# Two-layer conditional attention block on one core: the second layer's token eviction, ten groups' maxima and the last batch's tangent order move between ACT, DVE and Pool

## The chip, the cores and the metric

The kernel runs on one core of a Trainium2 chip. The metric is the device time of one execution in microseconds (us); the lower the better. The profile and the trace come from one profiled execution.

## What is computed

Four batches of 512 tokens with 256 channels pass through two attention layers of 16 heads (16 channels a head). Cut to what matters:

```python
# layer 0: RMS norm, modulation, rotary attention, output projection, residual
xn = x * rsqrt(mean(x * x) + eps) * rms_w
qkv = (xn * (1 + scale) + shift) @ w_qkv
x = softmax(rope(q) @ rope(k).T / 4) @ v @ w_out + x
# layer 1: layer norm, attention with a key mask, then a modulated second norm
xn = layer_norm(x, norm_w, norm_b)
y = softmax(q @ k.T + (1 - mask) * -1e6) @ v
e = silu(emb) @ emb_w + emb_b                      # scale, shift = halves of e
h = layer_norm(y, sb_norm_w, sb_norm_b) * (1 + scale) + shift
x = x + silu(h) @ out_w + out_b
```

`silu(h)` is computed as `(tanh(h/2) + 1) * (h/2)`. The change touches how `h/2` and `tanh(h/2)` are made for the four batches of the second layer.

## The kernel before, in words

**Steps and tiles.** The attention is cut into 32 groups (layer, batch, four heads): groups 0 to 15 are the first layer, 16 to 31 the second. Step s works on group s, and has four key tiles k = 0 to 3. Within a key tile the order of all engines is written out in `KEY_TILE`: the scores and the shifts of four heads (PE into one of four banks, ACT exponentiates into `probs`, L707), four row maxima of group s+2 (PE L524 makes row scores into one of three banks, DVE reduces them, L854 in the second layer), and the values product of the tile before (PE L541, eight records in a key tile). In key tile 1 PE also turns the maxima of group s+1 (L549), in key tile 2 it turns the output of group s-1 (L556), which DVE divides (L879, L881). Steps 30 and 31 have no row maxima, for there is no group 32.

**Rings.** What ACT evicts goes through the ring A of four banks, what DVE evicts through the ring D of three. A place in a ring is counted by `places()` in the order in which work is written out, and PE may fill the bank of a place once the place four (A) or three (D) before is evicted (`a_free`, `d_free`). All engines work through their own instructions in order.

**Pieces.** Other work is placed by hand in `PIECES`. In steps 22, 26 and 30, in key tiles 0 and 1, PE turns the normalised output tokens of batch 0, 1 and 2 of the second layer (`("turn", "f1", b, h)`, four transposes each, L576). Before the change they go into ring A, and ACT evicts each bank twice: with Identity into `halved` (L745, h/2), and with Tanh into `tanh` (L746), both with a scale and a bias per partition. (`halved` and `tanh` lie in the memory of `tables`, which is the name that the profile gives them.) Pool then makes `(tanh + 1) * halved` (L1245, L1247). PE projects it one step later (`y` pieces, L615), and DVE adds the residual (L903).

**Maxima to shifts.** Once the 16 maxima of a group are there, `negate` scales them by -1/64 and splits them into a high and a low part: on DVE in two instructions (L865, L867), on Pool in three (L1232, L1235, L1237). `POOL_SHIFTS` lists the groups for which Pool does it. The maxima of group n are complete at the end of step n-2; PE turns them in key tile 1 of step n-1, ACT copies them (L720), and DMA brings them to where step n uses them. In step 20, 24 and 28, key tile 3, DVE also takes the statistics of the output (L887, L892), and Pool makes the reciprocal deviation and the normalised tokens from them (L1089, L1091, L829).

**The last batch.** Behind the last step, batch 3 is done in two pairs p of token tiles by code of its own: ACT takes Tanh of each half bank (L789, four), DVE waits for each and then makes `halved` (L1024) and the product (L1027) from it, PE projects (L654), DVE adds (L1033). PE fills its waits with idle matmuls (L630).

Of the kernel before, what the change touches and what calls it, by code (L numbers as in the profile page):

```python
# [51 lines left out]
def spread(pieces):  # L52

    table = {}
    for step, by_tile in pieces.items():
        for k, names in enumerate(by_tile):
            table[step, k] = names
    return table
# [70 lines left out]

FIRST_BUSY = 14  # L130
LAST_BUSY = (14, 7)
PIECES = spread(PIECES)


# [20 lines left out]
TURNED = 1  # L155


POOL_SHIFTS = [23, 24, 25, 27, 28, 29, 31]


PARTS_AT = {-1: ((1, 0), (1, 1)), 0: ((1, 2), (1, 3)), 2: ((2, 0), (2, 1)), 3: ((2, 2), (2, 3)),
# [51 lines left out]
def places():  # L213

    a, d = {}, {}
    for entry in order():
        op = entry[0]
        if op == "score":
            a[entry] = len(a)
        if op == "maxima":  # L220
            a["shift", entry[1]] = len(a)
        if op in ("max", "output"):
            d[entry] = len(d)
        if op == "piece":
            ring = d if entry[1][0] in ("y", "modulate", "embed") else a
            ring[entry[1]] = len(ring)
    return a, d

# [12 lines left out]


def turned(use):
    return A[("turn",) + use + (CT - 1,)] + 1


def await_read(engine, q, use):
# [27 lines left out]
def columns(p):  # L275

    return slice(2 * p * P, (2 * p + 2) * P)
# [23 lines left out]
def build(nc, x, condT, mask, tables, vecs, w_cond, w_qkv, w_out, w_qkv1, v_b, emb_w, out_w, out_b, out):  # L301
# [4 lines left out]
    with ExitStack() as ctx:  # L306
# [67 lines left out]
        def sem(name):  # L374
            return ctx.enter_context(nc.semaphore(name))
# [20 lines left out]
        q.silu_made = sem("silu_made")  # L396
        q.tanh_step = sem("tanh_step")
        q.bias_step = sem("bias_step")
        q.halved_made = sem("halved_made")
        q.stat_step = sem("stat_step")  # L400
        q.p0_spread = sem("p0_spread")
        q.p0_moments = sem("p0_moments")
# [85 lines left out]
def tensor(nc, pe, m, q):  # L488

    def a_free(place):  # L490
        if place >= NA:
            pe.wait_ge(q.a_done, place - NA + 1)
        return a_bank(m, place)
# [64 lines left out]

    def turn_tokens(piece):
        _, kind, b, h = piece  # L560
        bank = a_free(A[piece])
        if kind == "f0":
            pe.wait_ge(q.d_done, D["output", NG * b + NG - 1] + 1)
            src = m.O[b % 2]
        else:
            n = NORMAL.index((kind, b))
            src = m.XN[n % 2]
            if h == 0 and n == 0:
                pe.wait_ge(q.ident_made, 4)
                pe.wait_ge(q.xn0_made, TPB)  # L570
            elif h == 0 and n == len(NORMAL) - 1:
                pe.wait_ge(q.xn0_made, 2 * TPB)
            elif h == 0:
                pe.wait_ge(q.xn_made, TPB * n)
        for t in range(TPB):
            last = nc.tensor.transpose(bank[:, t * P:(t + 1) * P], src[:, t, h * P:(h + 1) * P], m.ident[:, :])  # L576
        last.then_inc(q.a_made, 1)

    def queries_keys(piece):
        _, layer, b, i = piece  # L580
# [116 lines left out]
def scalar(act, m, q):  # L697
# [24 lines left out]
    def tokens(piece):  # L722
        _, kind, b, h = piece
        use = USES.index((kind, b))
        if use >= 2:
            await_read(act, q, use - 2)
        to = m.xT[use % 2][:, h, :]
        bank = made(A[piece])
        if kind == "p0":
            act.wait_ge(q.d_done, D["modulate",] + 1)  # L730
            act.wait_ge(q.mod_made, CT)
            act.activation(to, bank, ACT.Identity, bias=m.mod0_shift[:, h, b:b + 1], scale=m.mod0_scale[:, h, b:b + 1])\  # L732
                .then_inc(q.a_done, 1)
        if kind == "f0":
            act.activation(to, bank, ACT.Copy).then_inc(q.a_done, 1)
        if kind == "p1":
            act.activation(to, bank, ACT.Identity, bias=m.vecs[:, NORM_B + h:NORM_B + h + 1],
                           scale=m.vecs[:, NORM_W + h:NORM_W + h + 1]).then_inc(q.a_done, 1)
        if kind == "f1":
            act.wait_ge(q.mod1_step, 7)  # L740
            act.wait_ge(q.part_pool, 4 * (B - 1))
            if b:
                act.wait_ge(q.silu_made, CT * (b - 1) + h + 1)
            scale, bias = m.mod1[:, 0, h, b:b + 1], m.mod1[:, 1, h, b:b + 1]
            act.activation(m.halved[h], bank, ACT.Identity, bias=bias, scale=scale).then_inc(q.halved_made, 1)  # L745
            act.activation(m.tanh[h], bank, ACT.Tanh, bias=bias, scale=scale).then_inc(q.a_done, 1)  # L746

    def queries_keys(piece):
        _, layer, b, i = piece
# [30 lines left out]
    def last_batch():  # L780
        act.wait_ge(q.values_done, KT * GROUPS)
        act.wait_ge(q.d_made, D["output", GROUPS - 2] + 1)
        for p in range(PAIRS):
            act.activation(m.oT[:, columns(p)], m.ACC[:, columns(p)], ACT.Copy).then_inc(q.last_copied, 1)
        act.wait_ge(q.silu_made, CT * LAST)
        for p in range(PAIRS):
            act.wait_ge(q.last_tokens, p + 1)
            for h in range(CT):
                act.activation(m.tanh[h][:, columns(p)], m.a_banks[CT * p + h][:, 0:2 * P], ACT.Tanh,  # L789
                               bias=m.mod1[:, 1, h, LAST:B], scale=m.mod1[:, 0, h, LAST:B]).then_inc(q.last_tanh, 1)  # L790

# [41 lines left out]
def vector(dve, m, q):  # L833
# [139 lines left out]
    def modulate():  # L973
# [4 lines left out]
                              ALU.add, ALU.mult).then_inc(q.mod_made, 1)  # L978
        dve.tensor_copy(m.mod0_shift[:, :, :], bank[:, CT:2 * CT, :]).then_inc(q.d_done, 1)

    def embed(piece):
        c = piece[1]
        bank = made(D[piece])
        dve.tensor_scalar(m.e[:, c, :], bank[:, c * B:(c + 1) * B], 0.5, m.vecs[:, EMB_B + c:EMB_B + c + 1],
                          ALU.mult, ALU.add).then_inc(q.d_done, 1)

    def last_batch():
        O = m.O[LAST % 2]
        steps_done = TPB
        for p in range(PAIRS):  # L990
# [15 lines left out]
            for t in pair(p):  # L1006
# [3 lines left out]
            dve.wait_ge(q.last_step, steps_done)  # L1010
            dve.tensor_scalar(m.last_spread[:, at], m.last_moments[:, at, 1], 1e-5, None, ALU.add)\
               .then_inc(q.last_spread, 1)
        dve.wait_ge(q.a_made, turned(NORMAL[-3]))
        for t in range(TPB):
            dve.wait_ge(q.last_rstd, t // 2 + 1)
            dve.tensor_scalar(last_normal(m)[:, t, :], O[:, t, :], m.last_moments[:, t, 0:1], m.last_rstd[:, t:t + 1],
# [1 line left out]
        dve.wait_ge(q.mod1_step, 7)  # L1018
        dve.wait_ge(q.silu_made, CT * LAST)
        await_read(dve, q, len(USES) - 3)  # L1020
        for p in range(PAIRS):
            for h in range(CT):
                dve.wait_ge(q.last_tanh, CT * p + h + 1)
                dve.tensor_scalar(m.halved[h][:, columns(p)], m.a_banks[CT * p + h][:, 0:2 * P], m.mod1[:, 0, h, LAST:B],  # L1024
                                  m.mod1[:, 1, h, LAST:B], ALU.mult, ALU.add).then_inc(q.last_halved, 1)
                dve.wait_ge(q.last_halved, CT * p + h + 1)
                dve.scalar_tensor_tensor(last_tokens(m)[:, h, columns(p)], m.tanh[h][:, columns(p)], 1.0,  # L1027
                                         m.halved[h][:, columns(p)], ALU.add, ALU.mult).then_inc(q.last_silu, 1)
        dve.wait_ge(q.bias_added, B)
# [6 lines left out]
    for op, *at in order():  # L1036
        if op == "max":
            maximum(*at)
            n, j, h = at
            if (j, h) == (KT - 1, MAXED[-1]) and n not in POOL_SHIFTS:  # L1040
                negate(n)
        if op == "output":
            write_output(*at)
            if at[0] == GROUPS - 2:
                dve.wait_ge(q.d_done, D["output", GROUPS - 2] + 1)
                for t in range(TPB):
                    dve.bn_stats(m.last_stats[:, t, 0, :], m.O[LAST % 2][:, t, 0:EARLY]).then_inc(q.last_step, 1)
        if op == "statistics":
            take_statistics(*at)
        if op == "piece":  # L1050
            piece, = at
            if piece[0] == "y":
                residual(piece)
            if piece[0] == "embed":
                embed(piece)
    last_batch()
# [2 lines left out]
def silu_ready(engine, q, piece):  # L1059
    _, _, b, h = piece  # L1060
    use = USES.index(("f1", b))
    engine.wait_ge(q.a_done, A[piece] + 1)
    engine.wait_ge(q.halved_made, CT * b + h + 1)
    await_read(engine, q, use - 2)
    return use % 2, h


def gpsimd(pool, m, q):

    def normal(kind, b):  # L1070

        n = NORMAL.index((kind, b))
        if kind == "p0":
            pool.wait_ge(q.rstd0_made, b + 1)
        if n >= 2:
            pool.wait_ge(q.a_made, turned(NORMAL[n - 2]))
        src = m.O[b % 2] if kind == "f1" else m.X[:, TPB * b:TPB * b + TPB, :]
        for t in range(TPB):
            normal_tile(pool, m, kind, src, m.XN[n % 2], t, TPB * b + t).then_inc(q.xn_made, 1)
# [157 lines left out]
        pool.tensor_tensor(low, m.scaled[:, :, :, :], high, ALU.subtract).then_inc(q.pool_shift, 1)  # L1237

    for b in range(LAST):
        rstd("f1", b)  # L1240
        normal("f1", b)
        negate(NG * (B + b) + 7)
        for h in range(CT):
            i, h = silu_ready(pool, q, ("turn", "f1", b, h))
            pool.tensor_scalar(m.tanh[h], m.tanh[h], 1.0, None, ALU.add).then_inc(q.tanh_step, 1)  # L1245
            pool.wait_ge(q.tanh_step, CT * b + h + 1)
            pool.tensor_tensor(m.xT[i][:, h, :], m.tanh[h], m.halved[h], ALU.mult).then_inc(q.silu_made, 1)  # L1247
        for n in (NG * (B + b) + 8, NG * (B + b) + 9):
            if n in POOL_SHIFTS:
                negate(n)  # L1250
# [162 lines left out]
```

## Time and profile before

| | us |
|---|---|
| median of 3 runs | 519.7 (519.56 to 519.76) |
| the profiled execution's own time | 519.81 |
| its span in the trace | 518.0 |
| PE busy | 506.9 (98%) |
| DVE busy | 409.9 (79%) |
| ACT busy | 349.1 (67%) |
| Pool busy | 217.8 (42%) |

The granted clock of TensorE was 0.993 of full speed. Busy PE includes time in which a matmul only waits in the pipeline, so 98% doesn't say that PE sets the pace everywhere. The pace is read better from the start of each tile's values product to the start of the next.

### The profile page before, as it was taken

How to read it: one execution, taken by the hardware profiler on the slowest of the kernel's cores; microseconds unless marked ns; L12 is line 12 of the kernel's file. 1: busy time of each engine (PE TensorE's matmuls, PEld its weight loads, DVE VectorE, ACT ScalarE, POOL GpSimd, SP SyncE). 2: the span in 40 equal slices, each digit the busy share in tenths (PEclk: the TensorE clock that was granted, in tenths of full speed). 3: DMA queues.
4: the chain of work that ended last, by engine and by line, in shares of the span. 5: the costliest groups of instructions: out<-in, count | busy, mean ns of one | idle time of the engine just before them, and what ended most of it. 6: DMA issues, size and time to landing. Idle time of an engine off the chain costs nothing.

```text
span 518.0 us, 9855 instructions
## 1 busy us (share of the span) xinstructions
PE 506.9 (98%) x3346; PEld 195.2 (38%) x3346; DVE 409.9 (79%) x1059; ACT 349.1 (67%) x683; POOL 217.8 (42%) x244
## 2 busy tenths in 40 slices
PE   9999899999999999999999999999999999999987
PEld 5553422343433245333443344333333323332234
DVE  4876897998896788967898688966989998999026
ACT  1453467776667785866768685777787778777951
POOL 3039749999052420833146420832850044014401
PEclk8899999999999999999999999999999999999999
DMA  6983232332313033111321133110332112111011
GB/s 242 350 264 100 76 106 67 91 116 83 94 51 113 32 123 124 41 42 54 124 72 43 42 122 123 44 42 21 104 123 82 44 57 67 45 42 44 2 40 42
DMA packets 43034, 45.26 MB, mean 87 GB/s; under 512 B 4436, under 2 KB 41572, under 8 KB 42600
## 3 DMA queue, kind: packets, MB, share of 16 engines
q1 hardware_dynamic: 42696, 42.79, 26.4%
q10 hardware_dynamic: 288, 1.84, 0.9%
q8 instruction: 27, 0.44, 0.4%
q14 instruction: 23, 0.19, 0.1%
HBM read 25.46 MB, written 18.87 MB: 86 GB/s over the span
## 4 chain that ended last, share of the span: by engine, by line
PE 79%; DVE 9%; ACT 3%; issue 2%; POOL 1%; DVEq 0%; ACTq 0%
PE bank L541 20%; PE bank L524 12%; PE bank L515 10%; PE bank L504 9%; PE bank L587 9%; DVE masked L854 5%; PE bank L615 4%; PE bank L598 4%; PE bank L576 3%; PE bank L556 3%; ACT probs L707 2%; DVE row_max L857 1%; PE bank L549 1%; PE bank L623 1%; PE bank L654 1%
## 5 line engine op out<-in xcount | busy, mean ns | idle before, releaser
L707 ACT ACTIVATE probs<-bank 128x512 f32<-128x512 f32 x512 | 273.2, 603 | 83.3 <-PE bank L515 82.4
L857 DVE TENSOR_REDUCE row_max<-bank 128x1 f32<-128x512 f32 x256 | 162.9, 683 | 29.6 <-PE bank L524 27.9
L524 PE MATMUL bank<-k_s,q_s 64*128 64x512 f16 x512 | 183.2, 382 | 2.4 <-DVE row_max L857 1.2
L854 DVE CUSTOM_DVE_ANT_0 masked<-bank,mask_bias 128x512 bf16<-128x512 f32 x256 | 163.6, 686 | 16.0 <-PE bank L524 15.1
L504 PE MATMUL bank<-q_s,k_s 64*128 64x512 f16 x512 | 152.9, 381 | 2.0 <-ACT probs L707 1.0
L515 PE MATMUL bank<-shift,kx 64*128 64x512 f16 x512 | 149.2, 376 | 0.0
L541 PE MATMUL bank<-probs,v_aug 128*17 128x512 f32 x1024 | 135.4, 598 | 0.7 <-ACT probs L707 0.7
L524 PEld LDWEIGHTS bank<-k_s,q_s 64*128 64x128 f16 x512 | 46.1, 93 | 152.6 <-DVE row_max L854 67.8
L587 PE MATMUL bank<-xT,wqkv 128*128 128x512 f32 x128 | 61.7, 612 | 0.4 <-ACT xT L732 0.3
L515 PEld LDWEIGHTS bank<-shift,kx 64*128 64x128 f16 x512 | 46.6, 95 | 31.7
L504 PEld LDWEIGHTS bank<-q_s,k_s 64*128 64x128 f16 x512 | 31.8, 94 | 16.1 <-ACT probs L707 8.9
L587 PEld LDWEIGHTS bank<-xT,wqkv 128*128 128x128 f32 x128 | 22.3, 189 | 28.9 <-issue 25.0
L1089 POOL TENSOR_SCALAR spread<-moments_p 128x4 f32<-128x4 f32 x4 | 0.9, 229 | 72.8 <-DVE moments_p L892 72.8
L1101 POOL CAST parts<-plain 128x512 f16<-128x512 f32 x16 | 9.8, 610 | 51.6 <-ACT plain L758 51.6
L598 PE MATMUL bank<-wqkv,xT 128*128 128x256 f32 x128 | 31.3, 389 | 0.0
L541 PEld LDWEIGHTS bank<-probs,v_aug 128*17 128x17 f32 x1024 | 17.8, 95 | 33.6 <-issue 14.8
L615 PE MATMUL bank<-wo,xT 128*128 128x256 f32 x112 | 27.9, 392 | 0.0
L598 PEld LDWEIGHTS bank<-wqkv,xT 128*128 128x128 f32 x128 | 23.2, 190 | 8.6 <-issue 4.1
L879 DVE RECIPROCAL inv_sum<-bank 128x16 f32<-128x16 f32 x31 | 7.8, 252 | 21.5 <-PE bank L556 21.5
L1136 POOL TENSOR_SCALAR v_bias<-vb_row,vecs 128x256 f32<-128x256 f32 x16 | 14.8, 927 | 23.2 <-ACT v_tmp L772 22.4
L903 DVE TENSOR_TENSOR X<-bank,X 128x512 f32<-128x512 f32 x14 | 9.6, 686 | 18.8 <-PE bank L615 18.8
L615 PEld LDWEIGHTS bank<-wo,xT 128*128 128x128 f32 x112 | 20.1, 189 | 8.1 <-DVE row_max L854 2.5
(111 smaller groups left out, 507.3 us busy)
## 6 DMA issues: line engine op xcount, KB each, us to landing
q_parts<-parts SPq DMA_DIRECT2D x64, 128.0 KB
k_parts<-parts SPq DMA_DIRECT2D x64, 128.0 KB
q_s<-q_parts SPq DMA_DIRECT2D x32, 256.0 KB, 2.8
k_s<-k_parts SPq DMA_DIRECT2D x32, 256.0 KB, 3.0
X<-in_x SPq DMA_DIRECT2D x4, 512.0 KB, 7.4
y<-X SPq DMA_DIRECT2D x7, 256.0 KB, 2.7
wc<-in_w_cond ACTq DMA_DIRECT2D x1, 1024.0 KB, 5.2
tables<-in_tables SPq DMA_DIRECT2D x4, 256.0 KB, 7.1
```

The lines of the kernel that those rows point to most:

```text
L504: nc.tensor.matmul(bank, m.k_s[slot][rows, i, keys], m.q_s[slot][rows, i, :], start=True, stop=False)
L515: nc.tensor.matmul(a_bank(m, A["score", s, k, h]), keys, m.shift[s % SHIFTS][rows, i, :], start=False, stop=True).then_inc(q.a_made, 1)
L524: nc.tensor.matmul(bank, m.q_s[slot][rows, i, queries], m.k_s[slot][rows, i, :], start=True, stop=True).then_inc(q.d_made, 1)
L541: last = nc.tensor.matmul(m.ACC[W32 * h:W32 * h + W, :], m.v_aug[pu % VALUES][:, k, G * g + h, :], m.probs[k][:, h, :], start=(k == 0), st ...
L556: last = nc.tensor.transpose(bank[:, t * P:(t + 1) * P], m.oT[:, t * P:(t + 1) * P], m.ident[:, :])
L576: last = nc.tensor.transpose(bank[:, t * P:(t + 1) * P], src[:, t, h * P:(h + 1) * P], m.ident[:, :])
L587: last = nc.tensor.matmul(bank, m.wqkv[layer][:, k, i * P:(i + 1) * P], m.xT[use % 2][:, k, :], start=(k == 0), stop=(k == CT - 1))
L598: last = nc.tensor.matmul(bank[:, t * C:(t + 1) * C], m.xT[use % 2][:, k, at], m.wqkv[layer][:, k, 2 * C:3 * C], start=(k == 0), stop=(k = ...
L615: last = nc.tensor.matmul(bank[:, t * C:(t + 1) * C], m.xT[use % 2][:, k, at], m.wo[layer][:, k, :], start=(k == 0), stop=(k == CT - 1))
L707: act.activation(m.probs[k][:, h, :], bank, ACT.Exp, scale=1.0 if s >= B * NG else float(DH) ** -0.5)\
L854: dve.tensor_tensor_reduce(m.masked[D["max", n, k, h] % ND][:, :], bank, m.mask_bias[:, b, :], 1.0, LOWEST, ALU.add, ALU.max, to)\
L857: dve.tensor_reduce(to, bank, AX.X, ALU.max).then_inc(q.d_done, 1)
```

## The change

Three things: DVE evicts the turned tokens of batches 0 to 2 of the second layer (h/2 into SBUF) and ACT takes Tanh from that; Pool negates the maxima of groups 22 to 31, ten instead of seven (22, 26 and 30 are new), the one of group 4b+22 ahead of that batch's norm; and in the last batch the first `halved` is made before its Tanh, and products follow two `halved` at a time. The diff, cut to its core:

```diff
+LAST_HALVED = [(0, 1), (0, 0), (1, 0), (1, 1)]
-POOL_SHIFTS = [23, 24, 25, 27, 28, 29, 31]
+POOL_SHIFTS = list(range(22, GROUPS))
@@ places
-            ring = d if entry[1][0] in ("y", "modulate", "embed") else a
+            ring = d if entry[1][0] in ("y", "modulate", "embed") or entry[1][:2] == ("turn", "f1") else a
@@ tensor, turn_tokens
-        bank = a_free(A[piece])
+        bank = d_free(D[piece]) if kind == "f1" else a_free(A[piece])
...
-        last.then_inc(q.a_made, 1)
+        last.then_inc(q.d_made if kind == "f1" else q.a_made, 1)
@@ scalar, tokens
+        if kind == "f1":
+            act.wait_ge(q.d_done, D[piece] + 1)
+            if b:
+                act.wait_ge(q.silu_made, CT * (b - 1) + h + 1)
+            act.activation(m.tanh[h], m.halved[h], ACT.Tanh).then_inc(q.tanh_made, 1)
+            return
...
-        if kind == "f1":
-            act.wait_ge(q.mod1_step, 7)
-            act.wait_ge(q.part_pool, 4 * (B - 1))
-            if b:
-                act.wait_ge(q.silu_made, CT * (b - 1) + h + 1)
-            scale, bias = m.mod1[:, 0, h, b:b + 1], m.mod1[:, 1, h, b:b + 1]
-            act.activation(m.halved[h], bank, ACT.Identity, bias=bias, scale=scale).then_inc(q.halved_made, 1)
-            act.activation(m.tanh[h], bank, ACT.Tanh, bias=bias, scale=scale).then_inc(q.a_done, 1)
@@ scalar, last_batch
             for h in range(CT):
+                if (p, h) == LAST_HALVED[0]:
+                    act.wait_ge(q.last_halved, 1)
@@ vector
+    def halve(piece):
+        _, _, b, h = piece
+        bank = made(D[piece])
+        dve.wait_ge(q.mod1_step, 7)
+        dve.wait_ge(q.part_pool, 4 * (B - 1))
+        if b:
+            dve.wait_ge(q.silu_made, CT * (b - 1) + h + 1)
+        dve.tensor_scalar(m.halved[h], bank, m.mod1[:, 0, h, b:b + 1], m.mod1[:, 1, h, b:b + 1], ALU.mult, ALU.add)\
+           .then_inc(q.d_done, 1)
@@ vector, last_batch
+        dve.wait_ge(q.last_tokens, 1)
         for p in range(PAIRS):
-            for h in range(CT):
-                dve.wait_ge(q.last_tanh, CT * p + h + 1)
+            for _, h in LAST_HALVED[CT * p:CT * (p + 1)]:
+                if (p, h) != LAST_HALVED[0]:
+                    dve.wait_ge(q.last_tanh, CT * p + h + 1)
                 dve.tensor_scalar(m.halved[h][:, columns(p)], m.a_banks[CT * p + h][:, 0:2 * P], m.mod1[:, 0, h, LAST:B],
                                   m.mod1[:, 1, h, LAST:B], ALU.mult, ALU.add).then_inc(q.last_halved, 1)
-                dve.wait_ge(q.last_halved, CT * p + h + 1)
+            for h in range(CT):
+                dve.wait_ge(q.last_halved, CT * (p + 1))
+                dve.wait_ge(q.last_tanh, CT * p + h + 1)
                 dve.scalar_tensor_tensor(last_tokens(m)[:, h, columns(p)], m.tanh[h][:, columns(p)], 1.0,
                                          m.halved[h][:, columns(p)], ALU.add, ALU.mult).then_inc(q.last_silu, 1)
@@ gpsimd
     for b in range(LAST):
+        negate(NG * (B + b) + 6)
         rstd("f1", b)
         normal("f1", b)
```

## Rows read from the trace of the kernel before

**Rows 1.** The page's first line; a window around step 22: busy us by engine.

```profile
span 518.0 us, 9855 instructions
...
376.00:391.00 15.00, 14.64 (x117) 4.61 (x113) 13.30 (x43) 13.01 (x27) 7.37 (x8) 1.00 0.41 133
```

**Rows 2.** Waits, 370 to 505 us: who waited for whom, us in total, times, longest.

```profile
PEld bank L524 <- DVE row_max L854: 39.9, 80, 0.9
```

**Rows 3.** Timeline of PE: start us, us; the values product of successive tiles in four places.

```profile
369.51 1.05 PE L541 MATMUL bank<-probs,v_aug 128*17 128x512 f32 x8
...
372.47 1.08 PE L541 MATMUL bank<-probs,v_aug 128*17 128x512 f32 x8
...
378.08 1.05 PE L541 MATMUL bank<-probs,v_aug 128*17 128x512 f32 x8
...
381.15 1.05 PE L541 MATMUL bank<-probs,v_aug 128*17 128x512 f32 x8
...
384.73 1.05 PE L541 MATMUL bank<-probs,v_aug 128*17 128x512 f32 x8
...
388.32 1.05 PE L541 MATMUL bank<-probs,v_aug 128*17 128x512 f32 x8
...
405.71 1.05 PE L541 MATMUL bank<-probs,v_aug 128*17 128x512 f32 x8
...
408.21 1.08 PE L541 MATMUL bank<-probs,v_aug 128*17 128x512 f32 x8
...
411.33 1.05 PE L541 MATMUL bank<-probs,v_aug 128*17 128x512 f32 x8
...
418.55 1.05 PE L541 MATMUL bank<-probs,v_aug 128*17 128x512 f32 x8
...
421.65 1.08 PE L541 MATMUL bank<-probs,v_aug 128*17 128x512 f32 x8
```

**Rows 4.** Timeline of DVE and of PE behind the maxima of group 26.

```profile
418.21 0.37 DVE L865 TENSOR_SCALAR neg_max<-row_max 128x16 f16<-128x16 f32 x1
...
418.74 0.68 DVE L854 CUSTOM_DVE_ANT_0 masked<-bank,mask_bias 128x512 bf16<-128x512 f32 x1
...
420.71 0.39 PE L524 MATMUL bank<-k_s,q_s 64*128 64x512 f16 x1 [0.23 <-DVE row_max L854]
```

**Rows 5.** Timeline of Pool: the last bias before step 22, and the negation of group 24.

```profile
370.15 0.73 POOL L1139 TENSOR_TENSOR v_aug<-v_bias,v_tmp 128x256 f32<-128x256 f32 x1
...
380.27 0.27 POOL L1232 TENSOR_SCALAR scaled<-row_max 128x16 f32<-128x16 f32 x1 [3.13 <-DVE row_max L854]
...
380.89 0.22 POOL L1237 TENSOR_TENSOR neg_max<-scaled,neg_max 128x16 f16<-128x16 f32 x1
```

**Rows 6.** Timeline of ACT, DVE and PEld around the turned tokens of steps 22 and 30.

```profile
380.68 0.78 ACT L745 ACTIVATE tables<-bank,mod 128x512 f32<-128x512 f32 x1
...
383.18 0.69 DVE L854 CUSTOM_DVE_ANT_0 masked<-bank,mask_bias 128x512 bf16<-128x512 f32 x1
...
384.38 0.85 ACT L745 ACTIVATE tables<-bank,mod 128x512 f32<-128x512 f32 x1
...
385.71 1.16 ACT L707 ACTIVATE probs<-bank 128x512 f32<-128x512 f32 x2
...
482.64 0.84 ACT L745 ACTIVATE tables<-bank,mod 128x512 f32<-128x512 f32 x1
...
484.69 0.09 PEld L504 LDWEIGHTS bank<-q_s,k_s 64*128 64x128 f16 x1 [0.39 <-ACT probs L707]
```

**Rows 7.** Groups by line and shape: count, busy us, mean ns of one, idle before.

```profile
L707 ACT ACTIVATE probs<-bank 128x512 f32<-128x512 f32 x512 | 273.2, 603 | 83.3 <-PE bank L515 82.4
...
L1024 DVE TENSOR_SCALAR tables<-bank,mod 128x256 f32<-128x256 f32 x4 | 2.2, 538 | 0.3 <-ACT tables L789 0.3
...
L822 ACT ACTIVATE parts<-roped 128x512 f16<-128x512 f32 x4 | 2.5, 630 | 1.6 <-DVE roped L966 1.5
```

**Rows 8.** Timeline of the last batch.

```profile
508.57 0.73 DVE L1016 TENSOR_SCALAR XN<-O,last_moments,last_rstd 128x256 f32<-128x256 f32 x2 [0.27 <-POOL last_rstd L1254]
...
509.60 0.54 DVE L1024 TENSOR_SCALAR tables<-bank,mod 128x256 f32<-128x256 f32 x1 [0.29 <-ACT tables L789]
...
511.57 3.82 PE L654 MATMUL bank<-wo,xT 128*128 128x256 f32 x16 [0.26 <-DVE xT L1027]
```

More of the change, by code:

```diff
@@ L243, in turned, with await_turned @@
 def turned(use):
-    return A[("turn",) + use + (CT - 1,)] + 1
+    return (D if use[0] == "f1" else A)[("turn",) + use + (CT - 1,)] + 1
+def await_turned(engine, q, use):
+    engine.wait_ge(q.d_made if use[0] == "f1" else q.a_made, turned(use))
 def await_read(engine, q, use):
@@ L398, in build @@
         q.bias_step = sem("bias_step")
-        q.halved_made = sem("halved_made")
+        q.tanh_made = sem("tanh_made")
         q.stat_step = sem("stat_step")
@@ L724, in tokens @@
         use = USES.index((kind, b))
-        if use >= 2:
+        if use >= 2 and kind != "f1":
             await_read(act, q, use - 2)
         to = m.xT[use % 2][:, h, :]
+        if kind == "f1":
[4 more added lines that the diff above has]
+            return
         bank = made(A[piece])
@@ L1012, in last_batch @@
                .then_inc(q.last_spread, 1)
-        dve.wait_ge(q.a_made, turned(NORMAL[-3]))
+        await_turned(dve, q, NORMAL[-3])
         for t in range(TPB):
@@ L1053, in vector @@
                 residual(piece)
+            if piece[:2] == ("turn", "f1"):
+                halve(piece)
             if piece[0] == "embed":
@@ L1061, in silu_ready @@
     use = USES.index(("f1", b))
-    engine.wait_ge(q.a_done, A[piece] + 1)
-    engine.wait_ge(q.halved_made, CT * b + h + 1)
+    engine.wait_ge(q.tanh_made, CT * b + h + 1)
     await_read(engine, q, use - 2)
@@ L1075, in normal @@
         if n >= 2:
-            pool.wait_ge(q.a_made, turned(NORMAL[n - 2]))
+            await_turned(pool, q, NORMAL[n - 2])
         src = m.O[b % 2] if kind == "f1" else m.X[:, TPB * b:TPB * b + TPB, :]
```

## The prediction

> **What bounds the kernel now.** I read the shares of the engines first, then the waits, then PE's timeline tile by tile, and last the tail. In the 15 us around step 22 PE is busy for 14.64 us, DVE for 13.30 and ACT for 13.01 [rows 1]: three engines are near their limit, and none has much to give. The waits name the second-closest limit: PE's weight loads for row scores waited 80 times for a row maximum of DVE [rows 2]. Most of these waits lie under PE's own running matmuls and cost nothing, so I look at the pace itself, from one values product to the next [rows 3]. An undisturbed key tile with the turned maxima takes 2.50 us (405.71 to 408.21), one with the turned output 3.12 (to 411.33), and one with turned tokens 3.07 (378.08 to 381.15). Against these, time is lost in two kinds of place:
>
> - Behind a negation on DVE. The tile from 369.51 to 372.47 takes 2.96 us instead of 2.50, so 0.46 is lost (group 22). The tile from 418.55 to 421.65 takes 3.10, so 0.60 is lost (group 26). Group 30 lies in the same pattern 49 us later, and I take 0.60 for it too. That DVE is the cause shows in the row score that starts at 420.71, after PE had nothing to do for 0.23 us [rows 4].
> - Behind turned tokens on ACT. From 381.15 to 384.73 a tile with turned tokens and turned maxima takes 3.58 us, where 3.07 and 0.02 would be expected: 0.49 lost. From 384.73 to 388.32 it is 3.59 against 3.12 less some overlap: 0.47 to 0.49 lost [rows 3]. So some 0.97 us a step, in steps 22 and 26. In step 30 PE has no row scores, ACT is the slowest engine for the whole stretch, and nearly all of the ACT time of a piece is lost.
>
> **Part 1, three negations from DVE to Pool.** On DVE the one of group 26 occupies 418.21 to 418.74, when the next maximum starts [rows 4]; without it that maximum starts at least 0.53 us earlier, 0.65 with the wait for the group's own last maximum ahead of it. PE then finds its banks free on time: the row score of 420.71 needs the maximum that ended 0.06 us before; moved forward by 0.65 it would be ready at 420.06, and PE would want it at 420.20 by its undisturbed rhythm. So the loss of that tile goes whole: 0.60. The 0.33 us lost in the tile before it come from the statistics on DVE and stay. For group 22 the same step gives its 0.46. **Sum: 0.46 + 0.60 + 0.60 = 1.66 us.**
>
> What Pool pays: a chain of three instructions from 380.27 to the end of the third at 381.11, 0.84 us [rows 5]. For group 22 Pool is busy with the value bias until 370.88, so the negation is done at about 371.75. PE turns these maxima right ahead of the values product of 372.47, which moves to 372.01: a margin of 0.2 us, the smallest in the change. If it is missed, each tenth missed costs a tenth, and at most the 0.46 gained there. In batches 1 and 2 Pool was idle before. The norm of the tokens moves back by 0.9 us each time, and still ends over 1 us ahead of PE's transposes. No DMA is issued otherwise than before; the shifts' copies and transfers keep their places and move with PE.
>
> **Part 2, the tokens' eviction.** ACT loses two instructions with two pointer operands, whose starts lie 0.66 us apart (380.68, and the exponentials resume at 382.00, so 1.33 for both), and gets one Tanh without pointers. Of this kind is the exponential of 603 ns [rows 7], and its successor starts 0.50 after it. The trace has no Tanh from SBUF of that size. The ACT copy from SBUF took 630 ns [rows 7]; the bounds are 0.50 and the 0.66 of today's rows, and I take 0.50 as nearest in form.
>
> The Trainium skill (VectorE: DVE Perf Modes, section on the TRN2 errata) speaks against this swap of sources: it gives ScalarE 52 cycles more from SBUF than from PSUM, and VectorE 62 more from PSUM than from SBUF. The 630 against 603 ns agree in sign for ScalarE. By the rule the three Tanhs that sit on a path cost 0.04 us more each, and the sum below would be 0.1 us smaller.
>
> DVE's new instruction: tensor_scalar from PSUM with two pointers took 538 ns for 256 columns [rows 7]. For 512 the bounds are the 0.68 us of a maximum of this size [rows 4] and twice 538, 1.08. I add 0.26 for 256 more columns (residual adds of 512 against 256 columns differ so) and take 0.80, which occupies 0.73 of DVE's queue, 1.46 a step. That has cover: of the 15 us, DVE is idle for 1.7 [rows 1], and it lies in just these two tiles, where PE waits for ACT.
>
> ACT now waits for DVE, and the exponentials stand behind this wait. Step 22, first piece: DVE comes to it at 380.71, ends at 381.51, the Tanh starts at 381.57 and the exponentials at 382.07, against 382.00 before. So the first piece gains nothing on ACT. It does leave ring A one place emptier, so that a score needs the exponential four places back without the tokens in between; PE's stall in this tile goes. Second piece: DVE has a maximum at 383.18 [rows 6], comes to the piece at 383.79, ends at 384.59; the Tanh starts at 384.65, when ACT is free anyway, and the exponentials at 385.15 instead of 385.71 [rows 6]. PE's next stall is for the bank of the first of them (a score of the following tile), and moves forward by the same 0.55. I count 0.5 for step 22, 0.5 for step 26. What is late next is this one bank, 0.4 us of PE's waiting that stays.
>
> Step 30: DVE is idle, so it evicts at once. First piece: Tanh done by 480.13, before 480.25. Second: transposed at 481.62, evicted at 482.48, Tanh from 482.55 to 483.05; before, Identity began at 482.64 [rows 6] and the exponentials resumed at 483.96. That is 0.9; the score that waited until 484.69 [rows 6] starts at about 483.7. ACT paces the rest of the step at its old distance, so I take 1.0. **Sum: 0.5 + 0.5 + 1.0 = 2.0 us.**
>
> **Part 3, the last batch.** DVE began its chain at 509.60, when the first Tanh had ended [rows 8]; now it may start once its norms are done, at about 509.25 (508.57 and 0.73 less overlap) [rows 8]. The second `halved` follows at 509.71 and the products at 510.29 and 510.63, the latter done at 511.05, against 511.51. PE is then behind its idle matmuls until about 511.15 and starts the projection there instead of at 511.57 [rows 8]: 0.4. The 0.26 us for which PE waited between the two pairs [rows 8] goes at most, since DVE saves a dependent wait in each pair. Between 0.4 and 0.65, **I take 0.55 us.**
>
> **Sum:** 1.66 + 2.0 + 0.55 = 4.2 us. The profiled execution took 519.81 us, 1.8 more than its span [rows 1], and would take 515.6. The median of the runs shown is 519.7, 0.1 below it, so the forecast is 515.5.
>
> **Rivals.**
> - *DVE becomes the bound.* Between steps 21 and 23 the 1.46 us of new work meet 1.7 us of idle time; if that idle time isn't where it is needed, PE waits for row-score banks instead of score banks. For it: DVE had no gap before 382, and PE's waits for it are many [rows 2]. Against: ring D is not late in my schedule by more than 0.1 us at any place. It would take the 1.0 of steps 22 and 26 and cost up to 0.5 in each: 517.5. Chance 0.11.
> - *The negations were not what PE waited for,* but the 1.8 us of statistics ahead of them, and Pool's one for group 22 is late as well. Then part 1 gives 0 to 0.2: 517.1. Chance 0.04.
> - *Slower.* The place is ACT's wait for the tokens' eviction. Its price is DVE's backlog: with all three banks of ring D full ahead of the piece, DVE comes to it 1.83 us (3 x 0.61) after the transposes instead of 0.25, and the exponentials resume 1.6 us later than before. The four score banks cover some 0.65 of it, so 0.95 to 1.0 for each of six pieces, 6 us; with parts 1 and 3 gained, 519.7 + 6 - 2.2 = 523.5. It decides from a backlog of about 1 us (each piece must lose over 0.37). Against it: DVE is only some 0.25 us behind at 380.71, and idle in step 30. Chance 0.06.
> - *No difference.* PE's saved time is lost again at a wait that the trace doesn't show now, such as the shifts' or the operands' transfers: 519.3. Against it: shifts are turned 6 us before they are used. Chance 0.05.
>
> **How the numbers follow.** My forecast has 0.74. A difference of 0.2% (1.04 us) is about what a measurement of this kernel can tell from none. Faster: 0.74 + 0.11 + 0.04 = 0.89; same 0.05; slower 0.06. The range: below, the losses that I leave standing (0.4 in each of steps 22, 26 and 30) go too, 4.2 + 1.2 = 5.4 us, 514.3. Above it takes in the rival of DVE with its 517.5, and the slower `halved` of 1.08 us, which is less than that.
>
> **What would show it.** Right: tiles near 2.50 us behind the maxima of groups 22, 26 and 30; some 3.1 and 3.5 instead of 3.58 and 3.59 behind the tokens; a `halved` of about 0.80 us on DVE and a Tanh of 0.60 on ACT; the projection of the last batch starting 0.4 us earlier behind the values of the last step. Wrong: PE waiting for row maxima in steps 22 and 26, ACT idle for more than 0.9 us ahead of a Tanh, PE waiting for Pool at the turned maxima of group 22, or equal tiles with a time that didn't fall.

## The result and the profile after

| | before | after |
|---|---|---|
| median, same chip, us | 519.73 | 515.62 (515.57 to 515.79) |
| ratio, 95% interval | | 0.9921 [0.9909, 0.9933] |
| profiled execution, us | 519.81 | 515.57 |
| its span, us | 518.0 | 513.8 |

The change makes the kernel 0.8% faster: 4.1 us by the medians, 4.2 by the spans. The forecast was 515.5.

Timeline of PE after the change, where successive values products start. These answer to [rows 3], with every line number of the kernel moved by 8 or more:

```profile
377.83 1.05 PE L549 MATMUL bank<-probs,v_aug 128*17 128x512 f32 x8
...
380.92 1.05 PE L549 MATMUL bank<-probs,v_aug 128*17 128x512 f32 x8
...
384.10 1.08 PE L549 MATMUL bank<-probs,v_aug 128*17 128x512 f32 x8
...
387.52 1.05 PE L549 MATMUL bank<-probs,v_aug 128*17 128x512 f32 x8
...
417.65 1.05 PE L549 MATMUL bank<-probs,v_aug 128*17 128x512 f32 x8
...
420.15 1.08 PE L549 MATMUL bank<-probs,v_aug 128*17 128x512 f32 x8
```

The tile behind the maxima of group 26 takes 2.50 us (417.65 to 420.15), where it took 3.10. The two tiles with turned tokens behind the first take 3.18 and 3.42 us, where they took 3.58 and 3.59. Read in this way over the whole second layer, the gain has four parts:

| stretch | before | after | gained | forecast |
|---|---|---|---|---|
| tile behind the maxima of group 22, 26, 30 | 2.96, 3.10, 3.10 | 2.57, 2.50, 2.49 | 1.60 | 1.66 |
| steps 22 and 26, from the first turned tokens, five tiles each | 15.30, 15.21 | 14.65, 14.65 | 1.21 | 1.0 |
| step 30, five tiles | 14.30 | 13.34 | 0.96 | 1.0 |
| last values product to the end of the span | 15.23 | 14.66 | 0.57 | 0.55 |

They add up to 4.34 us. The trace after reached a values product of the second layer that lies ahead of everything changed (341.57 us in the one, 341.73 in the other) 0.16 us later; with it the spans' 4.2 us are complete.

Of the 1.21 us in the second row, 0.10 don't belong to the change. One tile of step 22 (390.80 to 393.38) takes 2.58 us in the trace of before, and 2.48 in the traces of two experiments below that keep its eviction (`e1_pool_only` and `e3_tail_only`). In the trace of before a weight load waits in it for the DMA that brings the keys, which is the likely cause, though no run shows it:

```profile
392.41 0.09 PEld L524 LDWEIGHTS bank<-k_s,q_s 64*128 64x128 f16 x1 [0.31 <-DMA k_s<-k_parts]
```

Timelines after the change of DVE, ACT and PEld around the turned tokens of step 22, which answer to [rows 6]:

```profile
379.85 0.69 DVE L862 CUSTOM_DVE_ANT_0 masked<-bank,mask_bias 128x512 bf16<-128x512 f32 x1
...
380.47 0.81 DVE L997 TENSOR_SCALAR tables<-bank,mod 128x512 f32<-128x512 f32 x1
...
383.63 0.81 DVE L997 TENSOR_SCALAR tables<-bank,mod 128x512 f32<-128x512 f32 x1
```

```profile
381.31 0.63 ACT L740 ACTIVATE tables<-tables 128x512 f32<-128x512 f32 x1 [0.76 <-DVE tables L997]
381.84 1.07 ACT L715 ACTIVATE probs<-bank 128x512 f32<-128x512 f32 x2
...
384.47 0.63 ACT L740 ACTIVATE tables<-tables 128x512 f32<-128x512 f32 x1
385.01 1.07 ACT L715 ACTIVATE probs<-bank 128x512 f32<-128x512 f32 x2
```

```profile
385.64 0.09 PEld L512 LDWEIGHTS bank<-q_s,k_s 64*128 64x128 f16 x1 [0.44 <-ACT probs L715]
```

ACT now idles for 0.76 us ahead of the first Tanh, which DVE releases. Ahead of the second it doesn't idle. The exponentials behind the second resume at 385.01, and the score that needs the bank of the first of them starts at 385.64: that wait of 0.44 us is what is left of the loss.

The windows of 15 us around step 22, in the columns of [rows 1]:

```profile
376.00:391.00 15.00, 14.86 (x119) 4.67 (x116) 14.85 (x47) 12.16 (x25) 8.52 (x9) 1.00 0.45 141
```

DVE is busy for 14.85 of 15 us, against 13.30. It is full, and yet it isn't what PE waits for in these tiles, as an experiment below shows.

The prices, by line and shape: one eviction on DVE, one Tanh from SBUF, then the three instructions of a negation on Pool:

```profile
L997 DVE TENSOR_SCALAR tables<-bank,mod 128x512 f32<-128x512 f32 x6 | 4.8, 808 | 2.2 <-PE bank L584 2.2
L740 ACT ACTIVATE tables<-tables 128x512 f32<-128x512 f32 x6 | 3.8, 635 | 2.3 <-DVE tables L997 2.1
...
L1256 POOL TENSOR_SCALAR scaled<-row_max 128x16 f32<-128x16 f32 x10 | 2.6, 259 | 63.9 <-DVE row_max L862 39.8 <-PE bank L523 24.0
L1261 POOL TENSOR_TENSOR neg_max<-scaled,neg_max 128x16 f16<-128x16 f32 x10 | 2.2, 222 | 0.9
...
L1259 POOL CAST neg_max<-scaled 128x16 f16<-128x16 f32 x10 | 2.0, 198 | 0.7
```

Pool and PE at group 22, the place with the smallest margin:

```profile
371.76 0.22 POOL L1261 TENSOR_TENSOR neg_max<-scaled,neg_max 128x16 f16<-128x16 f32 x1
```

```profile
372.16 0.23 PE L557 MATMUL bank<-ident,neg_max 128*32 128x128 f16 x1
```

Pool's part is done at 371.98, and PE turns it at 372.16: 0.18 us to spare.

The last batch after the change, from the timeline, which answers to [rows 8]:

```profile
505.60 0.99 DVE L1045 TENSOR_SCALAR tables<-bank,mod 128x256 f32<-128x256 f32 x2
...
506.17 1.48 ACT L797 ACTIVATE tables<-bank,mod 128x256 f32<-128x256 f32 x3 [0.34 <-DVE tables L1045]
...
507.52 3.63 PE L662 MATMUL bank<-wo,xT 128*128 128x256 f32 x16
```

The projection takes 3.63 us instead of 3.82, and the 0.26 us for which PE idled in [rows 8] is gone too. That idle time lay ahead of the projection and not between the two pairs, as the prediction took it: in the trace of before the idle matmuls end at 511.31 us (509.64 and 1.67), and the projection starts at 511.57.

```profile
509.64 1.67 PE L630 MATMUL bank<-idle 128*128 128x512 f16 x7
```

What PE lost between the pairs is the 0.19 us by which 3.82 exceeds 3.63.

### The profile page after: what moved, and what is told of

Read it like the earlier page. It is cut to its first block, busy times and chain, and to the rows that moved or that the text cites. A ratio compares the mean times of both kernels' runs of the same rounds, so it can differ in the third digit from the quotient of the medians.

```text
span 513.8 us, 9864 instructions
## 1 busy us (share of the span) xinstructions
PE 504.3 (98%) x3346; PEld 195.1 (38%) x3346; DVE 412.0 (80%) x1059; ACT 344.6 (67%) x677; POOL 220.4 (43%) x253
## 4 chain that ended last, share of the span: by engine, by line
PE 75%; DVE 11%; issue 2%; POOL 2%; ACT 2%; POOLq 0%; DVEq 0%; ACTq 0%
PE bank L549 19%; PE bank L532 12%; PE bank L523 10%; PE bank L595 9%; PE bank L512 9%; DVE masked L862 7%; PE bank L623 4%; PE bank L606 4%; PE bank L564 2%; PE bank L584 2%; ACT probs L715 1%; DVE row_max L865 1%; PE bank L557 1%; PE bank L631 1%; POOL XN L836 1%
## 5 line engine op out<-in xcount | busy, mean ns | idle before, releaser
L1256 POOL TENSOR_SCALAR scaled<-row_max 128x16 f32<-128x16 f32 x10 | 2.6, 259 | 63.9 <-DVE row_max L862 39.8
```

## The experiments

Times are medians; each was compared with the kernel before on the same chip, and the ratio to it is what counts. The changed kernel stands at 0.9921. For parts of less than 1 us I also read the tiles in the traces, which agree with each other to 0.02 us where the code is the same, but for the tile of 2.58 us above and one that I name below.

**The three parts alone.** First, the kernel before with the negations on Pool only:

```diff
-POOL_SHIFTS = [23, 24, 25, 27, 28, 29, 31]
+POOL_SHIFTS = list(range(22, GROUPS))
...
     for b in range(LAST):
+        negate(NG * (B + b) + 6)
         rstd("f1", b)
```

> The kernel before with only the three negations (groups 22, 26, 30) moved to Pool. My theory, that each was a stall of PE through DVE's late row maxima (0.46, 0.60 and 0.60 us): 1.6 us faster, 518.1 us, with tiles of 2.50 us where 2.96, 3.10 and 3.10 stood. Rival, that the statistics ahead of them were the cause: 0 to 0.3 us faster. The tiles with turned tokens stay at 3.58 and 3.59 us.

518.43 us, ratio 0.9974 [0.9963, 0.9984], so 1.35 us with an interval from 0.8 to 1.9. The timeline of PE:

```profile
380.70 1.05 PE L541 MATMUL bank<-probs,v_aug 128*17 128x512 f32 x8
...
384.28 1.05 PE L541 MATMUL bank<-probs,v_aug 128*17 128x512 f32 x8
...
387.87 1.05 PE L541 MATMUL bank<-probs,v_aug 128*17 128x512 f32 x8
...
418.00 1.05 PE L541 MATMUL bank<-probs,v_aug 128*17 128x512 f32 x8
...
420.50 1.08 PE L541 MATMUL bank<-probs,v_aug 128*17 128x512 f32 x8
```

2.50 us behind the maxima of group 26, and still 3.58 and 3.59 behind the tokens. The negations, not the statistics, cost the 0.6 us. The statistics' own tile stays at 2.81 us in all these kernels.

Second, only the eviction: the hunks of `places`, `turn_tokens`, `tokens` and `halve`, with `POOL_SHIFTS` and both `last_batch` as before.

> The kernel before with only the new eviction: DVE makes h/2 from ring D, ACT takes Tanh from it; negations and last batch as before. My theory: 2.0 to 2.2 us faster, 517.6 us, 0.6 us in each of steps 22 and 26 and 1.0 us in step 30; tiles of 3.10 us behind the maxima of groups 26 and 30 stay. Rival, that DVE is so full that this pays only once the negations have left it: under 1 us faster.

517.53 us, ratio 0.9959 [0.9946, 0.9971]: 2.1 us. Its tiles behind the tokens are 3.18 and 3.42 us, the same as in the changed kernel, and the one of group 26 stays at 3.09. So the two parts work each in its own place, and DVE had room for the eviction without the negations leaving.

Third, only the last batch: the hunks of both `last_batch`.

> The kernel before with only the new order in the last batch. My theory: 0.55 us faster, 519.2 us, with the projection's matmuls in one piece without the gap of 0.26 us and started 0.3 to 0.4 us sooner behind the transposes. Rival, that the output's transfers set the end: no change.

519.13 us, ratio 0.9988 [0.9979, 0.9997], 0.6 us. In its timeline of PE the projection again takes 3.63 us, where it took 3.82:

```profile
511.31 3.63 PE L655 MATMUL bank<-wo,xT 128*128 128x256 f32 x16
```

The last values product starts at 502.93 there and at 502.77 in the kernel before, whose projection starts at 511.57: 8.38 us against 8.80, 0.42 sooner. The stretch from that product to the end of the span falls from 15.23 to 14.67 us, so the transfers behind the projection don't set the end by themselves. The three ratios together give 0.9921, the changed kernel's own.

**Is it ACT's time or the free places in ring A?** The changed kernel, with the tokens in ring A but the same work on each engine:

```diff
-            ring = d if entry[1][0] in ("y", "modulate", "embed") or entry[1][:2] == ("turn", "f1") else a
+            ring = d if entry[1][0] in ("y", "modulate", "embed") else a
...
-        bank = d_free(D[piece]) if kind == "f1" else a_free(A[piece])
+        bank = a_free(A[piece])
...
-            act.wait_ge(q.d_done, D[piece] + 1)
+            act.wait_ge(q.halved_made, CT * b + h + 1)
...
-            act.activation(m.tanh[h], m.halved[h], ACT.Tanh).then_inc(q.tanh_made, 1)
+            act.activation(m.tanh[h], m.halved[h], ACT.Tanh).then_inc(q.a_done, 1)
```

> The changed kernel, but the turned tokens of the second layer stay in ring A: DVE still makes h/2 from that bank and ACT still takes Tanh from it, and the place comes free when the Tanh ends. It keeps the saving in ACT's time and takes away the four free places in ring A. If ACT's time is what pays (what PE waits for last is the bank of the first exponential behind the second Tanh, which comes at the same time in either ring): within 0.4 us of the changed kernel, 515.6 to 516.0 us. If the free places pay: 1.2 to 2 us slower than the changed kernel.

515.59 us, ratio 0.9923 [0.9911, 0.9936]. The tiles are 3.63 and 3.09 us instead of 3.18 and 3.42: the same stall, 0.12 us longer in all, one tile earlier. Over steps 22, 26 and 30 the tiles lose 0.12, 0.12 and 0.08 us, 0.3 in all, which the medians don't resolve. So of the eviction's 2.1 us, ring D is worth 0.3, and the rest is ACT's time.

**What DVE's latency costs.** The changed kernel with each eviction done twice:

```diff
+        dve.tensor_scalar(m.roped[1][h][:, :], bank, m.mod1[:, 0, h, b:b + 1], m.mod1[:, 1, h, b:b + 1], ALU.mult, ALU.add)
         dve.tensor_scalar(m.halved[h], bank, m.mod1[:, 0, h, b:b + 1], m.mod1[:, 1, h, b:b + 1], ALU.mult, ALU.add)\
            .then_inc(q.d_done, 1)
```

> The changed kernel, with DVE's eviction of the turned tokens done twice (the first into a spare tile), so that 0.73 us more of DVE lies ahead of each of the six Tanhs. If ACT's wait for DVE is on the path: 1.0 to 1.4 us slower in each of steps 22 and 26 and 0.7 us in step 30, 518.7 us. If DVE's work lies in idle time and ACT could wait: at most 0.5 us slower, 516.1 us.

519.38 us, ratio 0.9993 [0.9984, 1.0002]: the gain is gone. Timeline of ACT at step 22:

```profile
381.57 0.63 ACT L740 ACTIVATE tables<-tables 128x512 f32<-128x512 f32 x1 [1.48 <-DVE tables L998]
...
385.45 0.63 ACT L740 ACTIVATE tables<-tables 128x512 f32<-128x512 f32 x1 [0.81 <-DVE tables L998]
```

ACT idles for 1.48 us ahead of the first Tanh and 0.81 ahead of the second. The tiles are 3.90 and 4.13 us, 0.72 and 0.71 more than in the changed kernel, in step 26 too; step 30 loses 0.72 once, since there the second lies under ACT's other work, and the statistics' tile of step 28 takes 0.17 us more, for which I have no reason. Together 3.76 us, where 3.1 was expected. DVE's work ahead of the Tanh is on the path one for one in steps 22 and 26. This is the mechanism of the rival that ended slower, and 0.73 us more in each piece nearly reaches the time of before.

**The order on ACT.** The changed kernel with each Tanh behind the next two exponentials:

```diff
+    def tangent(piece):
...
+    late = []
     for op, *at in order():
         if op == "shift":
             exponential(*at)
+            if late and at[-1] == 3:
+                tangent(late.pop())
...
-            if piece[0] == "turn":
+            if piece[0] == "turn" and piece[1] == "f1":
+                late.append(piece)
+            elif piece[0] == "turn":
                 tokens(piece)
```

> The changed kernel, but in ACT's order each Tanh of the turned tokens stands behind the next two exponentials, so that ACT doesn't idle 0.55 to 0.76 us for DVE and PE's bank comes free sooner. If that idle time and the order are what is left of the loss: tiles of 3.42 us go to 3.10 us and 3.18 to 3.10 us, 0.8 us in steps 22 and 26 and up to 0.5 us in step 30, 514.4 us. If ACT's whole work in these tiles is the limit: no change. Pool gets its input up to 1 us later, which the projection a step later doesn't feel.

**514.12 us**, ratio 0.9895 [0.9881, 0.9908]: some 1.35 us less than the changed kernel by the ratios, 1.26 by the tiles. This beats both kernels. Timeline of PE, then of ACT:

```profile
380.73 1.05 PE L549 MATMUL bank<-probs,v_aug 128*17 128x512 f32 x8
...
383.90 1.08 PE L549 MATMUL bank<-probs,v_aug 128*17 128x512 f32 x8
...
387.05 1.05 PE L549 MATMUL bank<-probs,v_aug 128*17 128x512 f32 x8
```

```profile
381.57 0.63 ACT L735 ACTIVATE tables<-tables 128x512 f32<-128x512 f32 x1
...
384.67 0.63 ACT L735 ACTIVATE tables<-tables 128x512 f32<-128x512 f32 x1
```

No Tanh has idle time ahead of it any more, and the second tile takes 3.15 us, near the 3.12 of an undisturbed one with a turned output. With it goes the rival that DVE is the bound: DVE does the same work here. The shares came out otherwise than expected: steps 22 and 26 give 0.55 us together (0.8 expected, for the first tile stays at 3.17 us), and step 30 gives 0.72 (up to 0.5). In the window from 376 to 391 us PE is now busy for all of the 15.00 us and DVE for 14.96, so DVE has next to no room for more work there.

**The statistics.** The changed kernel with the statistics of batches 1 and 2 cut in two:

```diff
-for _b in range(B - 1):
-    STATISTICS[20 + NG * _b, 3] = ("f1", _b, None)
+STATISTICS[20, 3] = ("f1", 0, None)
+for _b in range(1, B - 1):
+    STATISTICS[20 + NG * _b, 3] = ("f1", _b, 0)
+    STATISTICS[21 + NG * _b, 0] = ("f1", _b, 1)
...
-            statistics(kind, b, lambda t: m.O[b % 2][:, t, :], 0, TPB)
+            statistics(kind, b, lambda t: m.O[b % 2][:, t, :], 2 * (j or 0), TPB if j is None else 2)
```

> The changed kernel, with the statistics of batches 1 and 2 of the second layer's output cut in two: two tiles in key tile 3, two in key tile 0 of the next step. If the 1.8 us burst on DVE causes the tiles of 2.81 us: 0.33 us less in each of two places, 515.0 us. Rival: the burst only moves the stall, or the norm on Pool becomes late: no change or slower.

516.91 us, ratio 0.9948 [0.9936, 0.9961]: slower than the changed kernel by 1.4 us. My expectation was wrong. Timeline of PE, then of DVE:

```profile
414.55 1.05 PE L551 MATMUL bank<-probs,v_aug 128*17 128x512 f32 x8
...
417.03 1.05 PE L551 MATMUL bank<-probs,v_aug 128*17 128x512 f32 x8
...
420.53 1.08 PE L551 MATMUL bank<-probs,v_aug 128*17 128x512 f32 x8
```

```profile
413.90 0.69 DVE L913 TENSOR_TENSOR X<-bank,X 128x512 f32<-128x512 f32 x1 [0.38 <-PE bank L625]
...
417.18 0.75 DVE L897 BATCH_NORM_STATS2 stats<-O 128x6 f32<-128x256 f32 x2
417.96 0.38 DVE L902 BATCH_NORM_AGGREGATE moments_f<-stats 128x2 f32<-128x6 f32 x4
```

The tile from 414.55 falls from 2.81 to 2.48 us, as expected, but the next one takes 3.50 instead of 2.50. In its old place the burst of 1.8 us lay largely beside the projection, for which PE needs 1.9 us of matmuls that ask nothing of DVE. Cut, it leaves DVE idle for 0.38 us there, and 1.1 us of it fall on a tile that has no such cover. Twice 1.01 less twice 0.33 are the 1.4 us.

> The later Tanh and the split statistics together on the changed kernel. They lie in different steps, so they should add: 2.0 us faster than the changed kernel, 513.7 us. If each fills the same slack: about the better of the two.

With the diffs of both: 515.66 us, ratio 0.9926 [0.9912, 0.9939]. The expected 513.7 us was missed by what the split costs. Against the split alone the later Tanh again gains 1.2 us by the tiles; the two do add, one with the wrong sign.

**Pool's order.** The changed kernel with the negation behind the norm:

```diff
     for b in range(LAST):
-        negate(NG * (B + b) + 6)
         rstd("f1", b)
         normal("f1", b)
+        negate(NG * (B + b) + 6)
```

> The changed kernel, with Pool's negation of groups 22, 26 and 30 behind the norm of the tokens instead of ahead of it. PE must then wait for Pool at the turned maxima: by Pool's rows some 5.9 us for group 22 (the norm ends near 377.0, the negation near 377.9, PE is there at 372.1) and 1.9 us for each of groups 26 and 30: 9.7 us slower, 525.3 us. If Pool's place in its order matters little: under 1 us.

529.73 us, ratio 1.0209 [1.0174, 1.0243]: 14 us slower than the changed kernel by the medians (15 by the ratios), more than the 9.7 expected. PE's timeline at group 22, the row of the waits, and windows at groups 22 (first two) and 26 (last three), in the columns of [rows 1], where the third number from the end is the granted clock:

```profile
379.43 0.27 PE L557 MATMUL bank<-ident,neg_max 128*32 128x128 f16 x1 [6.14 <-POOL neg_max L1261]
```

```profile
PE bank L557 <- POOL neg_max L1261: 10.4, 3, 6.1
```

```profile
369.00:379.40 10.40, 4.29 (x36) 1.32 (x33) 5.50 (x18) 4.97 (x10) 9.59 (x13) 0.80 0.08 28
379.40:385.20 5.80, 5.77 (x25) 1.57 (x25) 2.62 (x8) 1.64 (x4) 0.00 (x0) 0.50 0.37 106
...
430.00:432.40 2.40, 0.27 (x3) 0.10 (x2) 1.56 (x6) 1.32 (x3) 1.91 (x5) 1.00 0.00 0
432.40:437.00 4.60, 4.60 (x25) 1.44 (x24) 2.30 (x7) 1.43 (x4) 0.00 (x0) 0.63 0.34 104
437.00:440.00 3.00, 3.00 (x30) 0.86 (x28) 2.56 (x9) 2.35 (x5) 0.00 (x0) 1.00 0.56 196
```

The waits are near what was expected: 6.14 us here and 10.4 us over the three places, against 9.7. Nearly all of the rest is the clock. After the wait of 6.14 us the granted clock is 0.50, that is 1.2 GHz. PE is busy for 5.77 of the next 5.80 us, a row score takes 0.60 us instead of 0.39, and the tile with the turned output takes 5.67 us instead of 3.10. After the wait of 2.13 us at group 26 the clock is 0.63 on average over 4.6 us, and that tile takes 4.61 instead of 3.12; at group 30 it is 4.67. The three tiles behind the waits cost 5.6 us together. This profiled execution took 533.28 us, the slowest of its four, so these are its costs; the other three took 529.14 to 530.07, and which of the costs was smaller in them no trace shows.

**DVE copies for ACT.** The changed kernel with the later Tanh, and with DVE copying the accumulator of groups 29 and 30:

```diff
+DVE_COPIES = (29, 30)
...
-        if op == "values" and at[1] == KT - 1:
+        if op == "values" and at[1] == KT - 1 and at[0] not in DVE_COPIES:
             copy_output(at[0])
...
+        if op == "values" and at[1] == KT - 1 and at[0] in DVE_COPIES:
+            dve.wait_ge(q.values_done, KT * (at[0] + 1))
+            dve.wait_ge(q.d_made, D["output", at[0] - 1] + 1)
+            dve.tensor_copy(m.oT[:, :], m.ACC).then_inc(q.acc_copied, 1)
```

> The changed kernel with the later Tanh, and in steps 30 and 31, where DVE is idle and ACT sets the pace, DVE instead of ACT copies the values of groups 29 and 30 out of the accumulator. If ACT's work sets the pace there up to the first projection: 0.5 to 0.9 us faster than with the later Tanh alone, 513.4 us. If the copy's latency or PE is what counts: no change against it.

513.95 us, ratio 0.9891 [0.9875, 0.9908], not to be told from 0.9895. The 0.5 to 0.9 us that I expected didn't come. In the tiles the first copy gives 0.17 us and the second nothing: the tile in which it lies stays at 3.98 us, and ACT, which no longer copies there, waits for PE for 0.25 us.

## Why the prediction was right

**The negations** (1.66 us forecast, 1.60 in the tiles). The step that a maximum which starts 0.65 us earlier frees PE's bank in time held: 2.50 and 2.49 us, and the kernel with this part alone shows it by itself. At group 22 the tile is 2.57 and not 2.50, a gain of 0.39 for 0.46. The margin of 0.2 us that I gave Pool was 0.18, so Pool's part was done in time. The last 0.07 us lie between the turned maxima (372.16) and the values product (372.25), which in the tile of group 26 start 0.01 us apart; why stays open.

**The eviction** (2.0 forecast, 2.17 in the table, 2.07 without the 0.10 us that another tile lost before). DVE's 0.80 us was 0.808. The Tanh took 635 ns, near the 630 of the copy from SBUF and not the 603 from PSUM: by the Trainium skill (VectorE: DVE Perf Modes, the TRN2 errata) SBUF as a source costs ScalarE 52 cycles more, and the sign and the order of size agree with this trace, though Tanh and exponential differ in more than their source. The exponentials behind the Tanh follow it after 0.53 us, for 0.50 assumed. The first Tanh idled for DVE and gained nothing on ACT. The second gained the half microsecond (exponentials at 385.01, with PE 0.23 us ahead of the trace of before, against 385.71). Steps 22 and 26 gave 0.55 and 0.56 us for 0.5 each. In step 30 the exponentials behind the two Tanhs came at 477.47 and 480.38, with PE 2.67 us ahead: 480.14 and 483.05 on the clock of before, where the prediction had 480.13 and 483.05. One reason was told wrongly: I let the freer ring A remove a stall of PE. The kernel with the tokens in ring A shows that the freer ring mostly moves the stall to the other tile, where it is 0.12 us cheaper. The sum was right all the same, since I had taken it from the second piece's exponentials, which come at the same time in either ring.

**The last batch** (0.55 forecast, 0.57 measured). The projection starts 0.42 us sooner, for 0.4. The second term was misread: the 0.26 us of the row is PE's idle time ahead of the projection, which the 0.42 already holds, and it was counted as a gap between the pairs. What was lost there was 0.19 us. That the 0.15 us taken for it came out (0.57 less 0.42) is luck.

**The rivals.** DVE as the bound fell, although DVE is busy for 14.85 of 15 us: PE waits for the exponentials' bank, and when these come sooner, PE is faster with DVE's work unchanged. The rival that ends slower had the right mechanism and a sum whose terms were wrong. I let the four banks cover 0.65 us of a backlog in each of six pieces. The doubled eviction shows that 0.73 us more cost 0.72 in five pieces and nothing in the sixth, so beyond the changed kernel the banks cover nothing. That fits the trace, in which ACT already idles for the first Tanh and a bank is already late for PE. At this price the 1.58 us of backlog that the rival adds (1.83 less 0.25) would cost 7.9 us on top of 515.6. That is 523.5, the rival's own figure, which counted 6 us from the kernel before; that the two agree is chance. No run has that backlog, so this is an estimate. The rival that the statistics and not the negations were what PE waited for fell with `e1_pool_only`, which gains 1.6 us in the three tiles. The one that the time is lost again at another wait fell with the medians.

## What to carry to other kernels

Moving work off the engine that is waited for pays by the wait that ends last, and a hand-over between two engines adds a wait to the order of the second: put the dependent instruction behind work that is ready, as the later Tanh does for another 1.3 us. Work on a nearly full engine belongs where its consumer is busy with something else: the whole burst of statistics costs 0.33 us beside a projection, and part of it costs 1.01 in the next tile. A small step that is moved to a free engine must stand ahead of that engine's long work, or it isn't free at all: behind that work it cost 14 us here.

## What the runs showed that I had not expected

The price of a long wait of PE isn't the wait alone. After an idle stretch of 2.13 us the granted clock was 0.63 on average over the next 4.6 us, and the tile took 1.5 us more. The clock was still 1.00 in that wait, 0.89 in the first 1.2 us in which PE worked again, and 0.50 from 433.5 to 436.3 us, as windows of the same trace show:

```profile
432.30:433.50 1.20, 1.20 (x9) 0.22 (x9) 0.00 (x0) 0.27 (x1) 0.00 (x0) 0.89 0.00 0
433.50:436.30 2.80, 2.80 (x16) 1.14 (x14) 1.64 (x5) 1.09 (x2) 0.00 (x0) 0.50 0.31 93
```

After 6.14 us, in which it had already fallen to 0.50, it stayed there over 5.8 us, and the tile took 2.6 us more. The traces of before and after the change, in which PE waits for under 1 us at a time in these stretches, keep a granted clock of 1.00 there. The Trainium skill (TensorE: Matmul & The Clock Gate, part 1) says that a monitor of how busy the array has been sets the share of clock pulses let through; the 0.50 after 6.14 us without a matmul agrees.
